# Decoder layer (selective scan, cross-attention, experts): a slot table dealt out anew, with work moved between VectorE, ScalarE, TensorE and GpSimd

## The reference

```python
# 1: selective scan (mamba), d_inner 512, 16 states, chunks of 64 tokens
xc, res = split(x @ W_in.T + b_in)
u = silu(causal_conv3(xc) + conv_b)
dlt, Bm, Cm = split(u @ W_x.T)                 # 64, 16, 16 columns
delta = softplus(dlt @ W_dt.T + b_dt)
dA = exp(delta * A);  dBu = delta * Bm * u     # per token, channel, state
h[t] = dA[t] * h[t-1] + dBu[t]                 # from zero in each chunk of 64
y = (h * Cm).sum(states) * silu(res)
x = layernorm(x + y @ W_out.T + b_out)
# 2: cross-attention on ctx, 16 heads of 16 columns
q, k, v = x @ w_q.T + b_q, ctx @ w_k.T + b_k, ctx @ w_v.T + b_v
x = layernorm(x + softmax(q k.T / 4) v @ w_o.T + b_o)
# 3: eight experts, expert e takes 32 of every batch's 256 tokens
x = layernorm(x + (silu(x @ w1[e]) * (x @ w3[e])) @ w2[e])
```

## Time and the profile before

| | us |
|---|---|
| median of 3 runs | 3113.24 (3109.69 to 3125.89) |
| profiled execution, its own time | 3102.2 |
| its span | 3100.4 |
| first `w_piece` / second / thirty-second | 49.89 / 109.47 / 2356.66 |
| PE / DVE / ACT / POOL busy in the span | 2543.5 / 2235.6 / 1779.8 / 2116.9 |

### The profile page before, as it was taken

How to read it: one execution, slowest core, us unless ns; L and a number is a source line. 1 busy time by engine, 2 the same in 40 slices (tenths; PEclk the granted TensorE clock), 3 DMA queues, 4 the chain that set the end, 5 groups by cost and what they waited for, 6 DMA issues and landing times.

```text
span 3100.4 us, 49625 instructions
## 1 busy us (share of the span) xinstructions
PE 2543.5 (82%) x14784; PEld 1745.3 (56%) x14784; DVE 2235.6 (72%) x3682; ACT 1779.8 (57%) x3818; POOL 2116.9 (68%) x1064
## 2 busy tenths in 40 slices
PE   4578888788888888888888888888887768999997
PEld 3345655565555656565666656565655444555554
DVE  2778888888888888888888888888888731232222
ACT  2566767766766667666666667776666532122221
POOL 3999888988888888888888888998889600000000
PEclk8888999989999888998888989999998867999999
DMA  3355555555555555555555555555555340123111
GB/s 124 113 136 142 146 145 148 160 150 152 157 155 151 147 143 151 151 152 142 148 147 145 150 147 150 149 156 152 149 144 153 87 138 7 57 66 105 57 58 27
DMA packets 258282, 399.83 MB, mean 129 GB/s; under 512 B 49921, under 2 KB 190593, under 8 KB 253922
## 3 DMA queue, kind: packets, MB, share of 16 engines
q1 hardware_dynamic: 254434, 394.56, 46.1%
q10 hardware_dynamic: 3584, 2.10, 0.3%
HBM read 301.06 MB, written 94.37 MB: 128 GB/s over the span
## 4 chain that ended last, share of the span: by engine, by line
POOL 40%; PE 24%; issue 21%; ACT 6%; DVE 4%; DMA 3%; SPq 2%; ACTq 0%; POOLq 0%; DVEq 0%
POOL arena L488 21%; POOL arena L498 17%; PE g_ps L1260 5%; PE a_ps L840 5%; PE d_ps L1278 5%; PE u_ps L1260 4%; POOL u L479 2%; ACT dA_ps L564 2%; DMA arena<-w_dram 1%; PE y_ps L840 1%; DVE arena L699 1%; PE f_ps L840 1%; SPq L366 1%; ACT probs L603 1%; PE d_ps L1283 1%
## 5 line engine op out<-in xcount | busy, mean ns | idle before, releaser
L488 POOL TENSOR_TENSOR arena<-arena 128x1024 f32<-128x1024 f32 x512 | 1209.2, 2362 | 283.6 <-DMA arena<-w_dram 271.9
L564 ACT ACTIVATE dA_ps<-arena,a_neg 128x252 f32<-128x252 f32 x2048 | 875.1, 464 | 418.5 <-DVE dA_ps L722 173.5
L699 DVE TENSOR_TENSOR_SCAN arena<-dA_ps,arena 128x512 f32<-128x512 f32 x704 | 845.5, 1215 | 219.0 <-ACT dA_ps L564 211.5
L498 POOL TENSOR_TENSOR arena<-arena 128x512 f32<-128x512 f32 (+1 forms) x512 | 859.7, 1679 | 17.3 <-DVE arena L699 17.3
L603 ACT ACTIVATE probs<-st_ps 128x512 f32<-128x512 f32 x512 | 299.3, 585 | 227.4 <-PE st_ps L840 224.8
L699 DVE TENSOR_TENSOR_SCAN dA_ps<-dA_ps,arena 128x512 f32<-128x512 f32 x320 | 390.2, 1219 | 3.3 <-ACT dA_ps L564 3.2
L772 DVE TENSOR_REDUCE mx<-s_ps 128x2 f32<-128x512 f32 x512 | 344.0, 672 | 59.6 <-PE s_ps L840 58.6
L840 PE MATMUL a_ps<-xT,w_conv 128*128 128x256 f32 x1536 | 380.3, 399 | 0.0
L840 PE MATMUL y_ps<-arena,sel 128*32 128x256 f32 x4096 | 274.1, 413 | 87.5 <-POOL arena L498 87.5
L840 PE MATMUL s_ps<-k_st,q_st 96*128 96x256 f32 x1024 | 289.2, 366 | 57.5 <-DVE mx L772 44.0
L840 PEld LDWEIGHTS a_ps<-xT,w_conv 128*128 128x128 f32 x1536 | 295.3, 198 | 56.9 <-issue 16.4
(11 more groups left out here) (107 smaller groups left out, 3473.5 us busy)
## 6 DMA issues: line engine op xcount, KB each, us to landing
arena<-delta_dram SPq DMA_DIRECT2D x512, 128.0 KB, 3.0
arena<-w_dram SPq DMA_DIRECT2D x512, 128.0 KB, 3.4
arena<-bc_dram SPq DMA_DIRECT2D x128, 256.0 KB, 5.5
q_st<-q_parts_dram SPq DMA_DIRECT2D x512, 64.0 KB
k_st<-k_parts_dram SPq DMA_DIRECT2D x512, 64.0 KB
delta_dram<-delta SPq DMA_DIRECT2D x32, 512.0 KB, 3.8
w_dram<-u SPq DMA_DIRECT2D x32, 512.0 KB, 5.8
k_parts_dram<-parts SPq DMA_DIRECT2D x32, 512.0 KB, 3.4
```

The costliest lines, as they stand in the source:

```text
L488: pool.tensor_tensor(dBu[:, n % NB], w_r[:, n // RP % 2, t % RP].unsqueeze(1).to_broadcast([P, QS, L]), bc_r[:, b.par, 0], ALU.mult).then_ ...
L498: pool.tensor_tensor(h[:, n % NH, states], h[:, n % NH, states], bc_r[:, b.par, 1, states], ALU.mult).then_inc(s_hC, 1)
L564: last = nc.scalar.activation(dA[n % NDA][:, q, :, 1:], delta_r[:, n // (2 * RP) % 2, t % RP].rearrange("p (c t) -> p c t", t=CH)[:, :, 1: ...
L699: nc.vector.tensor_tensor_scan(dst, decays, dBu[:, n % NB, 2 * half:2 * half + 2].rearrange("p q t -> p (q t)"), 0.0, ALU.mult, ALU.add).t ...
```

## The change

What it does, part by part:

- `v_evac` goes from DVE to ACT as a plain copy; the bias of v is now a matmul of 4 rows (`bias[96:100]`) ahead of `v_proj`'s own, and the tile b_v and its load are gone.
- `max_parts` is split: `max_high` on ACT (copy with scale -1), `max_low` on DVE.
- HC_DVE has nine halves where it had ten, among them both halves of tile 10 (so POOL has no product for that tile) and half 0 of tiles 8 and 15. POOL has 8 products of 128x1024 and 7 of 128x512 per batch, where it had 6 and 10. The counter of scans is split in two, one for each half, so that halves may finish out of turn.
- `dBu_piece` and `hC_piece` on POOL stand one slot sooner, which moves them past `w_piece`; nothing else is in POOL's stream.
- The lists of all engines and many offsets are dealt out anew. In the first step SP now waits for the constants on DVE after the first of its ten weight loads. `load_experts` stands behind `load_stack(1)` of the last batch, where it was ahead of it.

```diff
-HC_DVE = [(0, 1), (1, 1), (2, 1), (3, 1), (4, 1), (6, 1), (9, 1), (12, 1), (13, 1), (14, 1)]
+HC_DVE = [(2, 1), (3, 1), (4, 1), (6, 1), (8, 0), (10, 0), (10, 1), (14, 1), (15, 0)]
...
                 for tile, name in weights:
                     sp.dma_start(tile, io[name]).then_inc(s_const, 16)
-                sp.dma_start(b_v[:], io["b_v"].partition_broadcast(P)).then_inc(s_const, 16)
-                sp.wait_ge(s_const_v, N_SET)
+                    sp.wait_ge(s_const_v, N_SET)
...
+                (O_REP + 8, replicate(3)),
+                (O_REP - 1, replicate(0)),
...
-                *[(O_SCAN + t - 1, dBu_piece(t)) for t in range(NU)],
-                *[(O_SCAN + t + 1, hC_piece(t)) for t in HC_POOL],
+                *[(O_SCAN + t - 2, dBu_piece(t)) for t in range(NU)],
+                *[(O_SCAN + t, hC_piece(t)) for t in HC_POOL],
...
                     if n >= NDA:
-                        act.wait_ge(s_scan, n - NDA + 1)
+                        act.wait_ge(s_scan[(n - NDA) % 2], (n - NDA) // 2 + 1)
...
+            def v_evac(b):
+                act.wait_ge(s_v_mm, b.value(TT, TT))
+                if b.back(2):
+                    act.wait_ge(s_pv, b.back(2).value(NG, NG))
+                nc.scalar.activation(v[:, b.par, :, :, 0:DK], f_ps[:].rearrange("p a (h i) -> p a h i", i=DK),
+                                     ACT.Copy).then_inc(s_v, 1)
...
+                    nc.scalar.activation(m_rows[:, gr % 2, 0], y_ps[0:HG * TT, L:], ACT.Copy,
+                                         scale=-1.0).then_inc(s_m_hi, 1)
...
+                (O_N1 - 6, norm(0, xt, s_mv1, s_ln1, s_x1)),
...
-                (O_N1 - 1, norm(0, xt, s_mv1, s_ln1, s_x1)),
...
-                nc.vector.tensor_tensor(v[:, b.par, :, :, 0:DK],
...
+                        mm(f_ps[:], bias[96:100, 2 * BC + P:2 * BC + 2 * P],
+                           bias[96:100, 0:D].unsqueeze(1).to_broadcast([4, TT, D]), True, False)
```

More of the change, by code:

```diff
@@ L57 @@
 O_SP = 11
-O_REP = 15
+O_REP = 16
 O_SCAN = 17
 O_OUT = 36
-O_N1 = 39
+O_N1 = 43
 O_K = 31
-O_X1T = 40
+O_X1T = 39
 O_Q = 43
 O_V = 44
-O_LD = 45
+O_LD = 48
 O_S = 48
@@ L268, in mixers @@
         s_dA, s_dBu = sem("dA_ready"), sem("dBu_ready")
-        s_scan, s_scan_v = sem("scan_done"), sem("scan_done_in_psum")
+        s_scan, s_scan_v = [sem(f"half_{i}_scanned") for i in range(2)], sem("scan_done_in_psum")
         s_hC, s_hC_v = sem("hC_done_pool"), sem("hC_done_dve")
@@ L437, in _ @@
             run_steps([
-                (0, load_x),
-                (O_K - 1, load_ctx),
[L440 to L452, removed]
+                (O_OF - 2, load_x1),
+                (O_SP + 2, w_store),
+                (O_XP + 2, bc_load),
+                (O_REP + 8, replicate(3)),
+                (O_REP - 1, replicate(0)),
+                (O_N1 - 2, store_x1),
+                *[(O_LD + HG * gr - 1, load_stack(gr)) for gr in range(NG)],
+                (O_REP + 3, replicate(1)),
+                (O_S + 3, load_experts),
+                (O_SP + 1, delta_store),
+                (O_Q + 3, store_parts(q_dram, s_q_hi, s_q_lo, s_q_dram)),
+                (O_OUT, load_x_tok),
+                (2, load_x),
+                (O_K + 7, store_parts(k_dram, s_k_hi, s_k_lo, s_k_dram)),
+                (O_REP + 7, replicate(2)),
+                (O_XP + 1, bc_store),
+                (O_N2 + 4, store_x2),
+                (O_K - 1, load_ctx),
             ], B)
@@ L620, in onT_evac, with max_high, piece @@
                 nc.scalar.activation(onT[:], a_ps[:], ACT.Copy).then_inc(s_onT, 1)
+            def max_high(gr):
+                def piece(b):
+                    act.wait_ge(s_mT_mm, b.value(NG, gr + 1))
+                    if gr >= 2:
+                        act.wait_ge(s_m_dram, b.value(NG * 16, 16 * (gr - 1)))
+                    else:
+                        if b.back(1):
+                            act.wait_ge(s_m_dram, b.back(1).value(NG * 16, 16 * (NG + gr - 1)))
+                    nc.scalar.activation(m_rows[:, gr % 2, 0], y_ps[0:HG * TT, L:], ACT.Copy,
+                                         scale=-1.0).then_inc(s_m_hi, 1)
+                return piece
             def max_store(gr):
@@ L817, in _ @@
             run_steps([
[L818 to L820 removed]
                 (O_K + 1, low(s_k_hi, s_k_lo)),
                 (O_OUT + 1, residual(0, xt, s_out_mm, a_ps, s_r1, s_st1, s_mv1, s_ln1, s_xtok)),
[L823 to L824 removed]
+                *[(O_ON + HG * gr + 1, head_norm(gr)) for gr in range(NG)],
+                (O_X1T + 2, x1T_evac),
                 (O_OF + 1, residual(1, r2, s_of_mm, a_ps, s_r2, s_st2, s_mv2, s_ln2, s_x1_ld)),
[L826 removed]
+                *[(O_SCAN + t, scan(t, 0)) for t in range(NU)],
                 (O_Q + 1, low(s_q_hi, s_q_lo)),
                 *[(O_S + hd + 1, row_max(hd)) for hd in range(H)],
+                *[(O_MT + HG * gr + 1, max_low(gr)) for gr in range(NG)],
                 *[(O_SCAN + t, scan(t, 1)) for t in range(NU)],
                 *[(O_SCAN + t, hC_piece(t, half)) for t, half in HC_DVE],
+                *[(O_SCAN + 4 * m + 6, gating(m)) for m in range(ND)],
                 *[(O_SCAN + t, clear_starts(t, half)) for t, half in HC_DVE],
@@ L1344, in layouts @@
     rows[96:98, 0:D], rows[96:98, D:2 * D], rows[96:98, 2 * D:2 * D + P] = i["attn_b_out"], i["xattn_b_o"], 1.0
+    rows[98:100, 0:D], rows[98:100, 2 * D + P:2 * D + 2 * P] = i["xattn_b_v"], 1.0
     return {
```

80 lines of the change are left out of this document (30 added, 50 removed).

## The result

The changed kernel takes 2942.62 us (median of 4 runs, 2936.04 to 2945.52), the kernel before 3118.48 us (4 runs); the ratio is 0.9434, 95% interval 0.9401 to 0.9468. The forecast was 2947 us.

The account below looks back on a forecast made before the run. POOL's 65.8 us of work and two transfers' place in SP's queue set the pace. 66.7 + 1.0 + 0 + 2.0 = 69.7 per period; 3102.2 - 161 + 5 - 10 = 2936, scaled 2947 us; range 2868 to 3088.

Parts of the forecast that it names:

- the two gaps: POOL's idle time ahead of the first and fifth product by B, awaiting replication parts: 2.85 and 5.09 us.
- term for DVE: In the pace: DVE alone would go at 67.4; POOL's waits for DVE go from 0.8 to 2.0 us per period.
- rival 1: The pace goes over to DVE, ACT and PE: POOL waits 5.7, period 72.4, median 3030 us; 18%.
- POOL's work: Products by C on POOL go from 26.9 to 27.8 us, making 66.7 us per period.
- Part 0: Replication transfer for the first product by B: follows w's landing at t0 + 6.1, lands t0 + 14.1; gap 1.0 us.
- t0: The end of w_piece on POOL, from which issue and landing times in a period are counted.
- The cover: POOL's work between w_piece and the first product by B: 14.2 us, was 16.7.
- Part 1: Replication transfer for the fifth product by B: issued t0 + 21.8, landed t0 + 29.8, hidden by 1 to 2 us.
- The start: Weights held until DVE's constants are set delay PE's first gate matmul: 5 us lost, between 0 and 10.
- The drain: PE's 13.44 us wait for a stack behind the experts' loads shrinks: 10 us gained, between 0 and 13.
- rival 3: Landings of both parts stretch behind earlier writes, by the completion-order rule: 3.8 us added to each, median 3039 us; 8%.
- The sum: Profiled 3102.2 - 161 + 5 - 10 = 2936 us, times 1.0035 gives 2946, rounded to 2947 us.

Follow-up runs that it names:

- e1: The kernel before with SP's list alone dealt out as in the changed kernel: 3024.56 us, ratio 0.9723.
- e2: The changed kernel with SP's list alone put back as before: 3202.34 us, ratio 1.0300.
- e3: The changed kernel with the products by B and C on POOL one slot later again, as before: 2943.92 us, ratio 0.9466.
- e12: The changed kernel with nine products on DVE on the same tiles, but half 1 instead of half 0 for tiles 8 and 15: 2904.11 us, ratio 0.9348.
- e13: The changed kernel with the old list of halves on DVE less (0, 1), so nine products: 2979.12 us, ratio 0.9592.
- e4: The changed kernel with the ten old halves on DVE, all half 1: 2994.19 us, ratio 0.9634.
- e5: The changed kernel with v's eviction (plain copy) and the negation of the maxima back on DVE: 2966.75 us, ratio 0.9565.
- e14: The changed kernel with products by B waiting for the scan alone and SP's constants wait behind all weight loads, as before: 2937.18 us, ratio 0.9450.
- e7: The changed kernel with the experts' loads ahead of the last batch's second stack again: 2939.99 us, ratio 0.9462.
- e11: e1 with products by B that wait for the scan alone, not for the clearing of the bank: 3022.02 us.
- e10: e4 with products by B that wait for the scan alone, not for the clearing of the bank: 2996.01 us.

## Why the prediction was right, and where its terms were off

- **What bounds the kernel.** Right: the two gaps closed when the queue was changed and came back when it was put back (e1, e2), with everything else equal. But that they end 8.4 us per period did not make them worth 8.4: alone, the queue gained 2.6, and POOL's waits for DVE took up 5.2 more (e1). The prediction had this in its term for DVE and in rival 1.
- **POOL's work**, 66.7 us per period: measured (2091.67 - 87.7) / 30 = 66.8.
- **Part 0.** The store of w, forecast at t0 + 0.3, went out at t0 + 0.03, and part 0, forecast at t0 + 6.1, at t0 + 6.1. In the second there is some luck: this store of w landed in 4.6 us (median of the kernel 4.1), not 5.8, and part 0 went out behind the load of ctx, at t0 + 5.6. The remaining gap of 1.0 us was 0.04. The cover that moving the products costs (2.5 us) was not needed: e3 gives it back and changes nothing.
- **Part 1**, issued at t0 + 21.8: measured 20.7, no gap. Right.
- **DVE.** 61.7 us of work: 60.6. Its idle time was taken as 5.7 us, and this step failed: the waits for decays and for the split of q and k did go (27.2 and 6.0 us in 30 periods, where they were 156.2 and 54.4), but DVE is idle 9.1 us per period, because of new waits, 115.2 us for PE's matmul of the attention heads and 57.5 for the negation on ACT. As it stands the sum has a slip besides: with both waits gone, 10.8 - 5.1 - 1.8 would have left 3.9. POOL's waits for DVE, taken as 2.0: measured 83.2 / 30 = 2.8. This term was mis-sized by 0.8 and the gap of part 0 by 1.0 the other way, so that the pace of 69.7 came out as 69.7 (69.72). That agreement to a tenth is luck; each of the two terms alone would have been off by 25 to 31 us in the time.
- **What the DVE term missed** is that the waits depend on which products stand where, and on TensorE's level at tile 11. The prediction priced the halves by their duration, 0.9 us for POOL and 0.7 for DVE. The same instructions on other halves are worth 38 us (e12), and the products of other tiles cost 36 (e13, nine of them) and 52 (e4, ten). Each is more than giving back v's eviction and the negation cost (24 us, e5).
- **The start.** 5 us taken for the weights: 6.2 at the gate, and right in mechanism (e14). The whole start, to the second `w_piece`, was 11.0 us longer; the other half comes from the parts of the change outside SP's list, since e2, with the old list, is at 123.61 us and e1, with the new one, at 110.48 (109.47 before). I had no term for it. The sum also took the gain per period 31 times; the first batch did not give it, and the 30 periods gave 155.5 us of the 161.
- **The drain.** The size, -10, was near the measured -12.2, and the cause was wrong: PE still waited 10.51 us for a stack, and with the old order of the loads the tail was 731.1 us, not longer (e7). Right number, wrong step; the cause stays open.
- **The rule against it** (rival 3). In the trace the 1 MB ahead of part 0 is issued by t0 + 5.6 and POOL waits 1.3 us for landings in 30 periods: no stretching that POOL waits for. One DMA of the replication of w lands in 3.2 us (median of 1200 to 1400), as before. The Trainium skill's rule on completion order ("DMA: Bandwidth & Descriptors", "Queues, rings and completion order") is neither borne out nor spoken against by this; no run here tests it. The store of w lands in 4.1 us (median of the whole span) where it took 5.8, and the store of delta in 5.9 where it took 3.8. The replication of B and C, which was issued between the two, is now issued ahead of both; that this is the cause was not tested.
- **The sum.** 2936 us was made against the profiled execution's own time, which came out as 2945.52, 10 us more. The scale to the median (1.0035) gave these 10 us back and was not there in the runs of the changed kernel, which lie at or below their profiled one. That 2947 and the median of 2942.62 differ by 4 us is luck; the pace of 69.7 and the closed gaps are what was foreseen. Of the rivals, rival 1 (DVE, ACT and PE take over the pace) comes near e1 and e11, the queue without the relief: 3025 and 3022 us against its 3030, a period of 72.3 against 72.4, though with POOL's work at 66.0 us and its waits at 6.4, not 66.7 and 5.7.

What stays open: how the 2.6 us per period between e1 and the changed kernel divide among halves, relief and lists. e4 alone accounts for 1.5 and e5 for 0.5, but the parts need not add up, as the queue's two prices show (e1, e2), and the computing engines' lists were not taken back one by one. Open is also what sets TensorE's level at the matmuls of q's projection: in both of the periods shown PE had stood 2.19 us for softplus (ACT, L555) a moment before.

## What to carry to other kernels

Read the queue of the issuing engine like any other engine's stream: find the transfer that the fullest engine waits for, and ask what stands ahead of it and what that waits for; here two transfers behind unrelated waits ended 8.4 of 74.9 us per period. Then ask what the engine will wait for next: closing these gaps alone gained 2.6 us. When two engines in a ring are both near full, a semaphore that is waited on is not by itself the cause: e10 and e11 removed waits of 73 and 146 us that were not needed and gained nothing, as the time was spent at the next one. When work is divided between them, count not only its duration but the instant at which its input is ready and how long it keeps a buffer: giving DVE the later half of two tiles was worth 1.1 us per period with the work unchanged. And follow a wait back through more than one engine: POOL's wait for DVE at tile 11 was DVE's for TensorE.

## What the runs showed of the hardware that was not expected

TensorE's mean granted clock went with the pace, with nothing done for it: 0.89 of 2.4 GHz in the periods of e2 (77.90 us), 0.91 before (74.91), 0.93 or 0.94 in e1, e4, e10, e13 and the changed kernel (72.34 to 69.72), 0.96 in e12 (68.60). Which of the two follows the other is not settled by the means; in single periods the clock's part can be seen, as the rows of 3.78 and 1.99 us above show. Beside it PE is busy as great a share of the changed kernel's periods as of e12's (1800 of 2092 us, 1769 of 2058, both 86%), so the busy share doesn't tell the two apart.

The scans' own duration does not go with that clock: for the same 128x512 form it is 1215 ns before and 1216 in e1 (clock 0.91 and 0.94), and 1207 in the changed kernel and 1208 in e2 (0.94 and 0.89). Why it changed was not looked into.
